# First expert blocks beside the last routing steps, with the block list behind unit 14 and a rearranged opening

## What is computed

```python
for l in (0, 1):
    x = x + tanh(g_xattn[l]) * cross_attention(layernorm(x), ctx)
    n = layernorm(x)
    top2, idx = top_k(n @ router_w[l], 2)
    # layer 0: h = silu(n @ w_gate[e]) * (n @ w_up[e]), hidden width 688
    # layer 1: h = relu(n @ w1[e]) ** 2,                hidden width 256
    # token t: sum over its two experts of weight * (h @ w_down[e])
    x = x + moe(n)          # x + tanh(g_ffn) * ... in both layers
```

## Time and profile before

| | us |
|---|---|
| median of 3 runs | 757.09 |
| lowest, highest | 756.56, 759.33 |
| the profiled execution | 756.57 |
| its span, first to last instruction | 754.8 |

### The profile page before, as it was taken

One profiled execution on the slowest core, in us unless ns is written; L12 is line 12 of the kernel. 1 busy time (PEld: TensorE's weight loads), 2 busy tenths in 40 slices (PEclk: granted clock), 3 DMA queues, 4 the chain that ended last, 5 costly groups with the idle time before them and its releaser, 6 DMA issues.

```text
span 754.8 us, 17644 instructions
## 1 busy us (share of the span) xinstructions
PE 684.7 (91%) x5904; PEld 517.5 (69%) x5904; DVE 414.9 (55%) x1385; ACT 273.9 (36%) x528; POOL 213.0 (28%) x399
## 2 busy tenths in 40 slices
PE   5798999989999999999999999979888898999970
PEld 3676777647777777777777777666666665778850
DVE  4677888853334333233233233369998987554426
ACT  2566566522112112112112112246655552445530
POOL 4122554471111111111111111112244556444440
PEclk9999999999999999999999999999999999999995
DMA  9033564461141131111101100241022232644429
GB/s 225 14 118 126 189 204 159 148 226 50 50 119 36 37 81 35 36 29 36 36 29 36 35 29 15 68 177 30 30 74 71 65 107 73 172 125 120 123 82 334
DMA packets 50857, 70.72 MB, mean 94 GB/s; under 512 B 7687, under 2 KB 38023, under 8 KB 50771
## 3 DMA queue, kind: packets, MB, share of 16 engines
q1 hardware_dynamic: 42380, 50.85, 22.5%
q0 software_dynamic: 6816, 18.69, 7.0%
q10 hardware_dynamic: 1575, 0.05, 0.2%
HBM read 46.55 MB, written 23.02 MB: 92 GB/s over the span
## 4 chain that ended last, share of the span: by engine, by line
PE 72%; DVE 16%; issue 5%; DMA 3%; POOL 2%; ACT 2%; DVEq 0%; POOLq 0%; SPq 0%; ACTq 0%
PE ps L1499 28%; PE ps L1529 17%; PE ps L1299 4%; PE ps L1512 3%; DVE m_rows L841 3%; DVE x_sb L825 3%; PE ps L1237 2%; PE ps L1312 2%; PE ps L1485 2%; PE ps L1265 2%; PE ps L1291 2%; PE ps L1254 2%; DVE ctx_q L858 2%; PE ps L1215 1%; DVE x_sb L875 1%
## 5 line engine op out<-in xcount | busy, mean ns | idle before, releaser
L1499 PE MATMUL ps<-w_all,share 128*128 x780 | 227.6, 439 | 2.7 <-DVE share L1118 2.7
L1499 PEld LDWEIGHTS ps<-w_all,share 128*128 128x128 f32 x780 | 144.2, 190 | 63.4 <-issue 5.2
L551 POOL DMA_INDIRECT ys_dram<-share,dest_i x78 | 75.4, 967 | 327.3 <-DVE share L1129 277.1
L1529 PE MATMUL ps<-w_all,share 112*128 (+1 forms) x624 | 148.0, 380 | 1.7 <-ACT share L737 1.0
L1529 PEld LDWEIGHTS ps<-w_all,share 112*128 112x128 f32 (+1 forms) x624 | 112.4, 190 | 15.1 <-issue 2.6
L1145 DVE TENSOR_TENSOR share<-share,ps 128x344 f32<-128x344 f32 x78 | 40.1, 514 | 138.6 <-PE ps L1499 77.4
L726 ACT COPY share<-ps 128x512 f32<-128x512 f32 x39 | 22.9, 586 | 152.0 <-PE ps L1512 152.0
L841 DVE TENSOR_REDUCE m_rows<-ps 128x8 f32<-128x960 f32 x64 | 70.4, 1139 | 11.2 <-PE ps L1254 11.1
L723 ACT ACTIVATE share<-ps 128x344 f32<-128x344 f32 x78 | 35.7, 458 | 104.5 <-PE ps L1499 104.5
L544 POOL DMA_INDIRECT xs_dram<-xn,slot_now x64 | 63.6, 994 | 21.4 <-issue 14.6
L514 POOL TENSOR_SCALAR nm<-mv 128x1 f32<-128x1 f32 (+1 forms) x48 | 12.1, 253 | 158.0 <-DVE mv L881 110.9
(11 more groups left out here) (204 smaller groups left out, 1005.0 us busy)
## 6 DMA issues: line engine op xcount, KB each, us to landing
share<-xs_dram SPq DMA_DIRECT2D x78, 129.0 KB, 2.1
w_all<-ys_dram SPq DMA_DIRECT2D x16, 512.0 KB, 7.0
w_all<-gate SPq DMA_DIRECT2D x8, 688.0 KB
w_all<-up SPq DMA_DIRECT2D x8, 688.0 KB
w_all<-down SPq DMA_DIRECT2D x8, 560.0 KB
w_all<-w SPq DMA_DIRECT2D x16, 256.0 KB
xs_dram<-q_flat SPq DMA_DIRECT2D x17, 129.0 KB, 2.6
out<-x_sb SPq DMA_DIRECT2D x8, 256.0 KB, 5.3
```

The lines of the kernel that those rows point to most:

```text
L551: g.indirect_dma_start(ys_dram, bass.IndirectOffsetOnAxis(ap=dest_i[:, u:u + 1], axis=0), y_sb[:, u, :], None).then_inc(D_y[u], 16)
L1499: i = t.matmul(ps[:, bank, 0:w], xgT[:, k, :], w_all[:, bass.ds(off + (k * UPW[l] + col - EW[l]), w)], start=(k == 0), stop=(k == KT - 1))
L1529: i = t.matmul(ps[:, 6, 0:D], hT[0:r, c + KD[1] * (j % 2) * l, :], w_all[0:r, bass.ds(off + (KT * UPW[l] + c * D - EW[l]), D)], start=(c = ...
```

## The change

EARLY goes from 6 to 5, so the first list covers 13 blocks and not 17. The list is made behind unit 14's division, inside the attention. Block 0's transposes and column copy stand in the last unit, and the routing's last steps stand between the parts of blocks 0 to 4. Of the 37 idle products behind the last unit's value products in each layer four are left; the six earlier in that unit became eight. GpSimd's last scatters alternate with the stores of the first blocks. SyncE loads two blocks, then expert 7 of layer 0, then the other blocks; the pad stores stand two to a load. A second expert load semaphore and separate PSUM and SBUF places for the last units go with it. In the opening the context is loaded ahead of x, eight products of the identity with itself run ahead of the keys, ScalarE loads its function table early, and the mask is split in three pieces, of which two go to units 1 and 3; the bias split goes to unit 0.

```diff
-    EARLY = 6
+    EARLY = 5
...
+            load_ctx(0)
             sp.dma_start(x_sb[:, 0:2, :], xv[:, 0:2, :]).then_inc(L_x[0], 16)
-            load_ctx(0)
...
-                for e in range(NE):
-                    sp.wait_ge(p_o, NU * l + min(1 + 2 * e, NU - 2))
+                for e in range(NE - 1 if l == 0 else NE):
+                    sp.wait_ge(p_o, NU * l + min(1 + 2 * e, NU - 3))
                     if l == 0 and e == NE - 2:
                         sp.wait_ge(p_k, 4)
                         sp.wait_ge(p_v, NB)
-                    if l == 0 and e == NE - 1:
-                        sp.wait_ge(p_pv[1], NU)
                     load_expert(sp, l, e)
...
                 sp.wait_ge(d_l1, 14 * (l + 1))
-                sp.wait_ge(*scattered(NB * l + EARLY - 2))
-                sp.wait_ge(*scattered(NB * l + EARLY - 1))
-                for j in range(U3):
+                for b in range(EARLY):
+                    sp.wait_ge(*scattered(NB * l + b))
+                sp.wait_ge(p_q, 2 * NB * (l + 1))
+                for j in range(2):
+                    load_block(j)
+                if l == 0:
+                    sp.wait_ge(p_pv[1], NU)
+                    load_expert(sp, 0, NE - 1)
+                sp.wait_ge(d_c, NU * (l + 1))
+                for j in range(2, N1 - 5):
                     load_block(j)
                 sp.wait_ge(d_pad, l + 1)
                 sp.wait_ge(g_z, 2 * l + 2)
                 for e in range(NE):
-                    load_block(U3 + e)
+                    if e % 2 == 0:
+                        load_block(N1 - 5 + e // 2)
                     row = sp.value_load(pad_i[0:1, e:e + 1], min_val=0, max_val=NE * REGION - P)
                     sp.dma_start(xs_dram[bass.ds(row, P), :], zrow).then_inc(D_pad, 16)
+                load_block(N1 - 1)
                 if l == 0:
...
-                for j in range(U3 + NE, N1):
-                    load_block(j)
                 sp.wait_ge(D_pad, 16 * (NE * (l + 1) + 1))
-                sp.wait_ge(*scattered(NB * l + NB - 2))
-                sp.wait_ge(*scattered(NB * l + NB - 1))
+                for b in range(EARLY, NB):
+                    sp.wait_ge(*scattered(NB * l + b))
                 sp.wait_ge(d_l2, 19 * (l + 1))
                 if l == 0:
                     load_ctx(0)
...
-                scatter(NB * l + NB - 2)
-                scatter(NB * l + NB - 1)
-                for j in range(BLOCKS):
+                B6, B7 = NB * l + NB - 2, NB * l + NB - 1
+                token_numbers(B6)
+                scatter_rows(B6, 0, 0)
+                scatter_rows(B6, 0, 1)
+                store_block(l, 0)
+                scatter_rows(B6, 1, 0)
+                store_block(l, 1)
+                scatter_rows(B6, 1, 1)
+                store_block(l, 2)
+                store_block(l, 3)
+                token_numbers(B7)
+                scatter_rows(B7, 0, 0)
+                store_block(l, 4)
+                scatter_rows(B7, 0, 1)
+                scatter_rows(B7, 1, 0)
+                store_block(l, 5)
+                scatter_rows(B7, 1, 1)
+                for j in range(6, BLOCKS):
                     store_block(l, j)
...
+            a.wait_ge(C_id, 2)
+            a.activation(first_act[:, :], ident[:, 0:1], ACT.Identity, scale=ident[:, 0:1])
...
+                    ctx_evac(0)
                     ln1_apply(B0)
-                    ctx_evac(0)
                     k_evac(0, 0)
+                    xnT_evac(B0, 2)
                     k_evac(0, 1)
-                    xnT_evac(B0, 2)
+                    q_evac(B0, (3, 1))
+                    ln1_apply(B0 + 1)
...
                         a.activation(act_sb[:, 344 * q:344 * q + 344], ps[:, 2 * q, 0:344], ACT.Silu).then_inc(e_act, 1)
+                    if j < 2:
+                        x2_evac(G1 - 1 + j)
                     a.wait_ge(b_hT, 2 * j + 1)
                     need(a, b_y, j)
                     a.copy(hT[:, 0:4, :], ps[:, 4, 0:4 * P].rearrange("p (c n) -> p c n", c=4)).then_inc(e_hT, 1)
+                    if first:
+                        ln2_apply(G1)
+                    if last:
...
-                    split_mask()
-                    v.wait_ge(L_mcol, 16)
-                    v.tensor_scalar(mask_col[0:K, :], mask_col[0:K, :], NEG, None, ALU.mult).then_inc(C_v, 2)
+                    split_mask(0)
                     ln1_stats(B0 + 1)
                     values(B0, 6)
-                    v.wait_ge(C_a, 1)
-                    split_bias(0)
...
+                    if l == 0 and u == 0:
+                        v.wait_ge(C_a, 1)
+                        split_bias(0)
+                    if l == 0 and u in (1, 3):
+                        split_mask(1 + u // 2)
                     divide(G)
...
+                    if u == NU - 2:
+                        list_full(0)
+                        list_full(1)
+                    if u == NU - 1:
+                        x_evac(0)
                 def list_rest(part):
...
+                def beside0(j):
+
+                    if j == 0:
+                        route2(B1 - 1)
+                        logits_copy(G1 - 1, LAST_LOGITS[l][1])
+                    if j == 1:
+                        logits_copy(G1, LAST_LOGITS[l][2])
+                        route1(B1)
+                        top_shift()
+                    if j == 2:
+                        route2(B1)
+                        counts_done()
+                    if 3 <= j <= 11:
+                        list_rest(j - 3)
+
+                def beside1(j):
+
+                    if j == 0:
+                        residual(G1)
+                        logits_copy(G1 - 2, LAST_LOGITS[l][0])
+                        route1(B1 - 1)
+                    if j == 1:
+                        route2(B1 - 1)
+                    if j == 2:
+                        logits_copy(G1 - 1, LAST_LOGITS[l][1])
+                    if j == 3:
+                        logits_copy(G1, LAST_LOGITS[l][2])
+                        route1(B1)
+                    if j == 4:
+                        route2(B1)
+                        counts_done()
+                    if j == 5:
+                        top_shift()
+                    if 5 <= j <= 7:
+                        for part in range(3):
+                            list_rest(3 * (j - 5) + part)
+                    if j == 8:
...
                 def blk0(j, u, first, last):
                     if first:
-                        x_evac(j)
+                        logits_copy(G1 - 2, LAST_LOGITS[l][0])
+                        route1(B1 - 1)
                     for q in range(2):
                         v.wait_ge(e_act, 2 * j + q + 1)
                         v.wait_ge(b_up, 4 * j + 2 * q + 2)
                         need(v, b_hT, 2 * j)
                         v.tensor_tensor(h_sb[:, 344 * q:344 * q + 344], act_sb[:, 344 * q:344 * q + 344],
                                         ps[:, 2 * q + 1, 0:344], ALU.mult).then_inc(e_h, 1)
+                    if first:
+                        residual(G1)
...
-                logits_copy(G0 + NU - 3, 5)
-                route1(B0 + NB - 2)
-                residual(G0 + NU - 1)
-                route2(B0 + NB - 2)
-                list_full()
-                logits_copy(G0 + NU - 2, 7)
-                logits_copy(G0 + NU - 1, 0)
-                route1(B0 + NB - 1)
-                top_shift()
-                route2(B0 + NB - 1)
-                v.wait_ge(d_cnt, 2 * l + 2)
-                v.tensor_tensor(pad_i[:, :], cnt[:, :], eR[:, :], ALU.add).then_inc(d_pad, 1)
-                v.wait_ge(d_cum, 2 * NB * (l + 1))
-                v.memset(cumb[:], 0.0)
-                v.wait_ge(d_l1, 14 * (l + 1))
+                    beside1(j)
+
                 run_blocks(l, (blk0, blk1)[l])
+                if l == 0:
+                    top_weights()
...
+                    def first_products(n):
+                        for _ in range(n):
+                            t.matmul(ps[:, 7, 0:2 * P].rearrange("p (j n) -> p j n", j=2), ident[:, :],
+                                     ident[:, :].unsqueeze(1).to_broadcast([P, 2, P]), start=True, stop=True)
+
+                    first_products(6)
                     ctx_t(0)
+                    first_products(2)
                     t.wait_ge(L_wk, 16)
                     k_proj(0, 0)
+                    x_t(B0, 2)
                     k_proj(0, 1)
-                    x_t(B0, 2)
...
+                    if u == 1:
+                        t.wait_ge(L_wo, 32 * (l + 1))
+                        t.wait_ge(C_bo, l + 1)
...
+                    if u == NU - 1:
+                        route(G - 2, LAST_LOGITS[l][0])
+                        idle_products(4, 2)
+                        block_t(0)
...
-                idle_products(2, 2)
-                route(G1 - 2, 5)
-                idle_products(3, 2)
-                x2_t(G1 - 1)
                 t.wait_ge(d_o, G1)
```

(49 more changed lines are left out.)

306 lines of the change are left out of this document (180 added, 126 removed).

## The result

| | before | after |
|---|---|---|
| median, us | 756.83 (4 runs) | 748.90 (4 runs) |
| lowest, highest | 756.25, 759.33 | 745.98, 751.08 |
| profiled execution, and its span | 756.57, 754.8 | 751.08, 749.3 |

The ratio is 0.9884, with a 95% interval of 0.986 to 0.9907: the change saves 8 us (7.0 to 10.6 by that interval), where 11.6 were forecast. The profiled execution of after is the slowest of its four. Each term is what a stage gained: TensorE's lead over the kernel before at the stage's end, less its lead at the end of the stage ahead of it. Before, layer 0's blocks 3 and 13 start their products at 186.65 and 267.65, in after at 176.30 and 263.87, in the second profile at 173.37 and 261.35.

The account below looks back on a forecast made before the run. TensorE, busy 91% of the span, was taken to bound the kernel, so holes in its queue count. 8.0 - 4.6 - 1.4 + 4.3 + 5.3 = 11.6 us, and 757.1 - 11.6 = 745.5; range 737 to 752.

Parts of the forecast that it names:

- forecast case: Whole kernel: the summed terms hold, 745.5 us, at 741 to 750; chance 0.50.
- (a): Rival: loads don't bind; block 13's load isn't held by the context, layer 1's pads are quicker; 737 us, chance 0.18.
- (c): Rival: the new start doesn't come, something holds block 0's rows or columns; gain 2, 755 us, chance 0.07.
- (d): Rival: TensorE's clock falls in layer 1's load-starved blocks 8 to 13 and stays down; 767 us, chance 0.05.
- Rival (b): VectorE's order costs more: routing in block 0, layer 1's list parts, mask pieces on the units' path; 751.5 us, chance 0.20.
- Layer 0's gap (8.0): Layer 0, last value products to block 3: first block 10.8 us earlier, block 3 about 8.0 earlier; bounds 6.8 to 9.
- VectorE decides block 0: Layer 0's first block: VectorE's chain sets its start, products at 153.4 in place of 164.17; the rows don't decide.
- Block 13 (-4.6, -1.4): Layer 0: rows queue behind context loads, TensorE stands still 4.6 us (bounds 1.0, 5.5); clock loss 1.4, half of 2.8.
- The opening (5.3): Start of layer 0: earlier and faster keys, hidden query wait, earlier first maximum, less a charge; 5.3 us, bounds 3.5 to 6.5.
- four gains: Opening: keys start earlier 1.6, upper clock level 2.8, query wait hidden 0.6, first maximum earlier 0.8 us.
- I charge 0.5: Opening: 0.5 us cost for bias split and two mask pieces in units 0, 1 and 3, where VectorE has holes.
- Layer 1 (4.3): Layer 1: first block 10.4 us earlier, less 2.85 for VectorE and 3.3 for SyncE's queue; net 4.3, bounds 1.5 to 8.

Follow-up runs that it names:

- second profile: Profile of the changed kernel, no edit, from a further set of six runs: span 745.9 us; the six runs' median is 749.61 us.
- mask_u2: Changed kernel with the second mask piece split in unit 2 of layer 0 in place of unit 1: 747.04 us, ratio 0.9874.
- the run meant for it: Changed kernel with layer 1's loads of blocks 8 and 9 ahead of the counts: 782.94 us, then 786.80 beside the changed kernel's 785.48.
- fills: Changed kernel with only idle products added, before unit 2's shifted scores in layer 0 and around block 0's transposes in both layers: 748.30 us, ratio 0.9874.
- again: The changed kernel once more, no edit: 749.61 us (6 runs), ratio 0.990 to the kernel before.
- ctx_later: Changed kernel with block 13's load issued ahead of layer 1's two context loads in layer 0: 742.57 us, ratio 0.9812.

## Why the prediction was right or wrong

**Right: the direction and the size.** 748.9 lies in the forecast case's own range of 741 to 750. The rivals don't fit: loads did bind (a), the new start came (c), and layer 1's clock didn't stay down (d). Rival (b) names a part of the miss, a mask piece on the units' path, but not the clock.

**Layer 0's gap (8.0).** 7.25 in the profile of after, 8.8 in the second; the difference is block 0 at the lower level. The products came 3.9 behind the value products (4.4 forecast), and block 0 to block 1 took 7.87 in the second profile (8.0). The transposes waited 0.41 and 0.36 for the rows, so the rows came last there by a little. The first products then waited 0.79 and 0.84 for VectorE's column copy; for this wait the prediction's claim that VectorE decides block 0 is true.

**Block 13 (-4.6, -1.4).** The best step. The hole was 4.67 (5.07 in the second profile), with the rows 7.8 us behind the list's end (7.6 forecast), and the clock behind it 1.4. That the 1.4 came out is luck: half of 2.8 was a guess on whether the level falls. It fell each time, and costs 1.4 in full, since behind this hole the lower level lasted some 3.4 us (0.66, 0.50 and 0.99 over three stretches of 2 us), not as long as in the opening. The Trainium skill's warning of idle gaps (TensorE: Matmul & The Clock Gate, "Why this matters for your kernels") bore on this place as it was weighed; the trace agrees (0.66 and 0.50 behind the hole).

**The opening (5.3).** The first shifted scores, in before and in after, are 6.0 us apart:

```profile
27.86 0.62 PE L1265 MATMUL ps<-q_flat,w_all 32*120 32x256 f32 x8
...
21.84 0.62 PE L1374 MATMUL ps<-q_flat,w_all 32*120 32x256 f32 x8
```

The prediction's four gains made 5.8 before its charge. Two sizes were off and cancelled by luck: the fillers are worth about 1.6, not 2.8, because only the key half that comes first would have been slow, and the order gave some 4.4 where 3.0 were forecast. The step that failed here is "I charge 0.5" for the mask and the bias. It cites VectorE's hole before one maximum, but the piece in unit 1 had no hole beside it. It took 1.5 in both profiles, by `mask_u2`, and another 1.6 in the one where the clock fell behind it.

**Layer 1 (4.3).** Block 0 was 10.5 us earlier (10.4). Between blocks 0 and 13 the second profile has 35.96 us, where 35.4 were forecast, so the working of VectorE's stalls and SyncE's queue holds as a sum. In that profile SyncE issues block 8, the last of nine loads in one row, 15.7 behind block 0 (14.7 to 15.6), and then a load every 3.4, as forecast:

```profile
622.34 19.92 SPq L415 DMA_DIRECT2D share<-xs_dram  x9
...
645.32 0.36 SPq L415 DMA_DIRECT2D share<-xs_dram  x1
...
648.71 0.36 SPq L415 DMA_DIRECT2D share<-xs_dram  x1
```

The profile of after has 38.7: 1.7 is the clock in block 0, and the loads come every 3.7 to 3.9. Its two waits for VectorE's list parts are 0.66 and 1.00 (1.2 forecast for both). What the queue alone is worth wasn't shown: the run meant for it moved the delay to the pads, in a group where the changed kernel didn't wait for rows there.

**The miss of 3.7 us (11.6 forecast, 7.9 measured).** About 2 us of it are the clock, which was charged at block 13 only. By the line through the executions the lower median clock costs 3.5 us, of which 1.4 were in the sum. Waits shorter than block 13's were taken as safe, because one of 1.32 us had left the level alone: one wait in one execution, read as a rule. In the executions since, short holes at unit 2 and at both block 0s cost the level in some and not in others, 1.5 to 1.7 us a place in the profile of after. The prediction also left layer 1's attention out. The kernel before loses the level there once in its profile. The changed one loses it once in after and in `fills`, and twice in `again`, `ctx_later` and `mask_u2`, the second time 34 us behind the first.

The other 2 us aren't the clock. At equal clock the kernels differ by 11.1 us, and that has to be held against 13.0, the sum without its 1.4 for the clock. The mask piece in unit 1 took 1.0 more than was charged; the rest is spread over small terms that one profile doesn't settle.

Which holes lower the mean clock isn't shown. The second profile, whose mean clock (0.978) is close to the median's, loses nothing at either block 0 and nothing at unit 2: what it loses beyond the kernel before is block 13's fall and the second one in layer 1's attention. Filling the other holes brought 1.3 us, within the scatter. When a short hole costs the level, and why layer 1's attention loses it in both kernels, stays open.

## What to carry to other kernels

Where a change takes filler work away, price every place with a hole for the clock, each as a chance times the loss read from rows at both levels, and look at several executions: here the span of an execution went with its mean clock, and the profile of after alone priced the short holes at 5.0 us, of which filling them brought 1.3. A load that the next stage needs goes ahead of bulk loads for a later one, even when both become possible at the same moment; moving two lines behind block 13's load gave 7.0 us. Before moving vector work "into the units", read whether that very unit has a hole, not its neighbour.

## What was not expected of the hardware

- In the opening the granted clock reads 1.00 while products take nearly twice as long as later: four key products took 3.54 us in the kernel without the first products, and 1.85 in the changed one. The stretch of the former:

```profile
8.00:10.00 2.00, 1.68 (x2) 0.84 (x3) 0.00 (x0) 1.05 (x3) 1.54 (x7) 1.00 1.13 322
```

- The kernel before took about 757 us in one group of runs and 796 and 795 in two others, one of them on a chip of the same number. Single instructions of VectorE and ScalarE last the same in both. In the slower groups the engines stop for what the profile can't name, or puts down to another core or an unknown queue ("remote"). In a profile of the changed kernel TensorE's waits are, in us in total, times and longest:

```profile
PE ps L1400 <- issue: 6.2, 4, 1.9
```

and the page has for ScalarE's exponentials (busy, mean ns, idle before, and what ended most of it):

```profile
L695 ACT ACTIVATE share<-ps,mask_col 120x1024 f32<-120x1024 f32 x32 | 33.9, 1110 | 45.2 <-remote 24.8
```
